# Stack loads of a two-pass attention kernel split by heads into two groups

## The reference

```
q_rot, k_rot = _rotate(q, cos, sin), _rotate(k, cos, sin)          # 16 heads of 8 channels
scores = einsum('bhqd,bhkd->bhqk', q_rot, k_rot) / sqrt(8) + decay_bias
scores = where(causal, scores, -inf)
attn = softmax(scores); out = einsum('bhqk,bhkd->bhqd', attn, v) @ Wo.T
```

## Time and profile before

| what | value |
|---|---|
| median of 3 runs | 1439.15 us (1437.37 to 1440.41) |
| profiled execution | 1432.54 us, span 1430.7 us |
| TensorE busy | 1284.3 us (90%) |
| VectorE busy | 1021.5 us (71%) |
| ScalarE busy | 762.4 us (53%) |
| GpSimd busy | 221.6 us (15%) |
| share of the 16 DMA engines, queue q1 | 32.6% |
| granted TensorE clock, mean | 0.984 of 2.4 GHz |

### The profile page before, as it was taken

One profiled execution on the slowest core, in us unless ns is written; L12 is line 12 of the kernel. 1 busy time (PEld: TensorE's weight loads), 2 busy tenths in 40 slices (PEclk: granted clock), 3 DMA queues, 4 the chain that ended last, 5 costly groups with the idle time before them and its releaser, 6 DMA issues.

```text
span 1430.7 us, 33751 instructions
## 1 busy us (share of the span) xinstructions
PE 1284.3 (90%) x10686; PEld 1016.5 (71%) x10780; DVE 1021.5 (71%) x3882; ACT 762.4 (53%) x1664; POOL 221.6 (15%) x326
## 2 busy tenths in 40 slices
PE   0369999999999999999999999999999979999999
PEld 0247777777778777777777777777777767777776
DVE  8557777777777777777777777777776656677754
ACT  1125655665555555555555555555555574455532
POOL 4011112111122211111111111112111200000000
PEclk9679999999999999999999999999999999999999
DMA  4423233223333333333222233223223204554344
GB/s 117 94 54 85 76 77 76 75 76 80 79 85 79 78 76 79 83 90 90 77 75 76 75 83 80 76 75 76 75 76 77 58 9 172 204 202 153 149 153 159
DMA packets 89904, 133.33 MB, mean 93 GB/s; under 512 B 9675, under 2 KB 78395, under 8 KB 78523
## 3 DMA queue, kind: packets, MB, share of 16 engines
q1 hardware_dynamic: 89298, 132.10, 32.6%
q10 hardware_dynamic: 488, 0.01, 0.0%
HBM read 108.76 MB, written 21.50 MB: 91 GB/s over the span
## 4 chain that ended last, share of the span: by engine, by line
PE 63%; DVE 15%; DMA 11%; issue 6%; ACT 4%; DVEq 1%; SPq 0%; ACTq 0%
DMA qst<-mT 10%; PE ps L1663 8%; PE ps L1649 8%; PE ps L1401 7%; PE ps L1402 6%; PE ps L1411 6%; PE ps L1275 4%; PE ps L1379 4%; DVE mx L1025 3%; PE ps L1337 3%; PE ps L1360 3%; PE ps L1333 2%; PE ps L1330 2%; PE ps L1436 1%; PE ps L1383 1%
## 5 line engine op out<-in xcount | busy, mean ns | idle before, releaser
L629 ACT ACTIVATE pr<-ps 128x512 f32<-128x512 f32 x384 | 227.7, 593 | 205.4 <-PE ps L1360 166.7
L1025 DVE TENSOR_REDUCE mx<-ps 128x2 f32<-128x512 f32 (+1 forms) x384 | 263.9, 688 | 46.6 <-PE ps L1330 26.2
L634 ACT ACTIVATE ps<-trn 128x512 f32<-128x512 bf16 x382 | 229.8, 601 | 12.1
L530 POOL TENSOR_TENSOR n1s<-rep,n1T 128x256 f32<-128x256 f32 x256 | 177.0, 730 | 277.4 <-DVE mpart L1037 252.9
L1663 PEld LDWEIGHTS ps<-w2s,ats 128*128 128x128 f32 x1024 | 131.7, 192 | 50.4 <-issue 46.5
L1401 PE MATMUL ps<-n1s,wq 128*128 128x256 f32 x512 | 160.6, 396 | 0.0
L1402 PE MATMUL ps<-n1s,wk 128*128 128x256 f32 x512 | 152.8, 380 | 0.0
L1411 PE MATMUL ps<-wv,n1s 128*128 128x128 f32 x1024 | 150.6, 280 | 0.0
L803 ACT ACTIVATE n1s<-ps 128x512 f32<-128x512 f32 x128 | 76.5, 597 | 123.3 <-PE ps L1649 122.1
L1411 PEld LDWEIGHTS ps<-wv,n1s 128*128 128x128 f32 x1024 | 131.9, 192 | 9.0 <-issue 6.3
L1663 PE MATMUL ps<-w2s,ats 128*128 128x128 f32 x1024 | 135.7, 276 | 1.1 <-DVE ats L1207 1.1
(11 more groups left out here) (225 smaller groups left out, 2281.6 us busy)
## 6 DMA issues: line engine op xcount, KB each, us to landing
rep<-scr_rw SPq DMA_DIRECT2D x32, 1024.0 KB, 5.0
qst<-scr_rw SPq DMA_DIRECT2D x16, 1024.0 KB, 6.5
kst<-scr_rw SPq DMA_DIRECT2D x16, 1024.0 KB, 8.3
scr_parts<-parts SPq DMA_DIRECT2D x64, 192.0 KB, 2.3
qst<-scr_parts SPq DMA_DIRECT2D x192, 64.0 KB
kst<-scr_parts SPq DMA_DIRECT2D x32, 192.0 KB
xt<-in_x SPq DMA_DIRECT2D x32, 128.0 KB, 2.3
kst<-scr_parts SPq DMA_DIRECT2D x32, 128.0 KB
```

Of the source, the lines that this page charges most:

```text
L530: pool.tensor_tensor(n1s[:, e], rep[:, par, e], n1T[:, par], ALU.mult).then_inc(n1s_done, 1)
L629: act.activation(pr[:, G % 2, i], ps[:, S2[k % 2]], ACT.Exp).then_inc(exp_done, 1)
L634: act.activation(ps[:, S2[k % 2]], seeds[:, 1 if (k + 2) % 3 == 2 else 0], ACT.Copy).then_inc(seed_done, 1)
L1025: dve.tensor_reduce(mx[:, min(i, 1), h:h + n], ps[:, S1[k % 2]].rearrange("p (h t) -> p h t", h=n), AX_X, ALU.max, negate=True).then_inc(s ...
```

## The change

`stacks` gets an argument `half` and issues the ten DMAs for 8 of the 16 heads. It is called twice in a row: for half 0 it waits until 6 units of pass 2 of batch n are done, for half 1 until all 12 are. Each half counts on a semaphore of its own; `unit1` waits for half 0 at unit 0 and for half 1 at unit 6. All rows of a load are 4 KB now. Nothing is changed in what the other engines do.

```diff
 Q_SLOTS = ((0, 1, 0), (1, 1, 0), (2, 1, 0), (3, 1, 1), (4, 1, 1), (5, 1, 2))
 K_SLOTS = ((0, 3, 0), (3, 2, 0), (5, 1, 0))
 KR = P
+HALF_HEADS = H // 2
 STACK_DMAS = 1 + len(Q_SLOTS) + len(K_SLOTS)
 LN2_LINKS = 3 + 10
...
         rot_chain = sem("rot_chain")
         parts_out = sem("parts_out")
         parts_stored = sem("parts_stored")
-        stack_in = sem("stack_in")
+        stack_in = [sem("stack_lo_in"), sem("stack_hi_in")]
         v_out = sem("v_out")
         v_done = sem("v_done")
         s1_out = sem("s1_out")
...
                     sp_.dma_start(scr_parts[par, side].rearrange("p d h t -> (d h) p t"),
                                   parts[:, :, side]).then_inc(parts_stored, 16)
-            def stacks(b, par, old):
+            def stacks(b, par, old, half):
+                hh = slice(HALF_HEADS * half, HALF_HEADS * (half + 1))
                 if old:
-                    sp_.wait_ge(s2_out, UNITS * (b - 1))
-                sp_.dma_start(qst[R_MAX:R_MAX + 3, par], zeros_b[:].broadcast_to((3, H, S))).then_inc(stack_in, 16)
+                    sp_.wait_ge(s2_out, UNITS * (b - 2) + UNITS // 2 * (half + 1))
+                sp_.dma_start(qst[R_MAX:R_MAX + 3, par, hh], zeros_b[:].broadcast_to((3, HALF_HEADS, S))
+                              ).then_inc(stack_in[half], 16)
                 sp_.wait_ge(parts_stored, 32 * (b + 1))
                 for side, dst, slots in ((0, qst, Q_SLOTS), (1, kst, K_SLOTS)):
-                    v = scr_parts[par, side].rearrange("p d h t -> (p d) (h t)")
+                    v = scr_parts[par, side].rearrange("p d h t -> (p d) h t")
                     for first, n, part in slots:
-                        rows = dst[R_PARTS + DH * first:R_PARTS + DH * (first + n), par].rearrange("p h t -> p (h t)")
-                        sp_.dma_start(rows, v[DH * part:DH * (part + n)]).then_inc(stack_in, 16)
+                        rows = dst[R_PARTS + DH * first:R_PARTS + DH * (first + n), par, hh]
+                        sp_.dma_start(rows, v[DH * part:DH * (part + n), hh]).then_inc(stack_in[half], 16)
             def store_weights(b, par):
...
                 if n_x >= 2:
                     store_parts(n + 2, u)
                 if n_x >= 2:
-                    stacks(n + 2, u, True)
+                    stacks(n + 2, u, True, 0)
+                    stacks(n + 2, u, True, 1)
                     store_weights(n + 2, u)
                 if n_x:
                     put_max(n + 1, 1 - u)
             store_parts(0, 0)
-            stacks(0, 0, False)
+            stacks(0, 0, False, 0)
+            stacks(0, 0, False, 1)
             store_weights(0, 0)
             spread_weights(0, 0)
...
             sp_.wait_ge(x_in, 32)
             load_x(2, 0, xt, x_in)
             store_parts(1, 1)
-            stacks(1, 1, False)
+            stacks(1, 1, False, 0)
+            stacks(1, 1, False, 1)
             store_weights(1, 1)
             put_max(0, 0)
             step(0, 0, 3)
...
                     pe.wait_ge(rwT_done, b + 1 if not isinstance(b, int) or b else 2)
                 if k == 0:
-                    pe.wait_ge(stack_in, 16 * STACK_DMAS * (b + 1 if not isinstance(b, int) or b else 2))
+                    pe.wait_ge(stack_in[0], 16 * STACK_DMAS * (b + 1 if not isinstance(b, int) or b else 2))
+                if k == UNITS // 2:
+                    pe.wait_ge(stack_in[1], 16 * STACK_DMAS * (b + 1 if not isinstance(b, int) or b else 2))
                 if k == 0:
                     pe.wait_ge(mT_done, b)
```

## The result

The changed kernel takes 1394.6 us (median of 4 runs, 1393.7 to 1394.73) where the kernel before, run beside it, took 1438.26 (1435.13 to 1440.41): a ratio of 0.9714, 95% interval [0.9692, 0.9736], 43.7 us less. The forecast was 1411, with a range that ended at 1403. The direction and the place were right; the gain was 28 us in the forecast and 43.7 in fact. Later groups of runs of the kernel before had medians of 1434.4 to 1437.3, so some 4 of the 43.7 us can be scatter of that kernel; against the lowest of them the gain is 39.8.

What follows compares the result with a forecast made beforehand. TensorE, busy 90%, bounds the kernel, with idle time before pass 2 while `put_max` waits behind stack loads. Gains of 26.0 (loop) and 2.0 (start) make 28.0 us, taking the median 1439.15 to 1411; range 1403 to 1424.

Steps and rivals of the forecast that it cites:

- Item 1, the mechanism: End of pass 2: with half the stack bytes left there, their tail ends before `put_max` is issued, hiding its landing.
- Item 1, the size: TensorE's wait ahead of pass 2: 28 steps at 0.93 us each, a gain of 26.0 us; ends 0 and 26.
- the two steps that I used as steps without a stop: Loop steps of 33.31 and 33.05 us, read as without idle time, 0.96 shorter than the average 34.14.
- Item 2: Low half's earlier issue on SP: its waits and loads fit in 4.3 us of idle queue; cost 0.
- Item 3: TensorE's waits in `unit1` for the two halves: both landed a step earlier in the steady loop; cost 0.
- Item 4, the start: Pass 1 of batch 0 waits for the low half alone: gain of 2.0 us taken, ends 2.4 gain and 2.4 loss.
- The sum: Whole kernel: 26.0 + 2.0 = 28.0 us gain; profiled execution 1432.54 becomes 1404.5, median 1439.15 becomes 1411.
- the 6.6 us: Excess of the kernel before's three-run median, 1439.15 us, over its profiled execution; its place was not seen.
- A: Rival: the tail shrinks less or another late thing takes half the gap; 13 us gain, 1426 us; chance 0.08.
- B: Rival: stack-load time is per load, not per byte, so `put_max` lands as now; forecast 1440 us; chance 0.07.
- C: Rival: SP's issue of loads cut by heads gets dearer, delaying `put_max`; 17 us more, 1456 us; chance 0.05.
- The rule that speaks against it: Stack loads: transfers under 64 KB are dominated by per-descriptor cost, so 32 KB loads would bring the sum near 0.

Runs made afterwards that it cites:

- the second trace of before: The kernel before, unchanged, profiled once more: profiled execution 1436.01 us, median of nine runs 1434.42 us.
- the run made for it: Kernel before with twelve whole, late stack loads, each load's rows spread six partitions apart: 1446.23 us, ratio 1.0087.

## Why the prediction was right and wrong

- *Item 1, the mechanism.* Right. The tail of the stack loads held `put_max`; half of the bytes end before it is issued; TensorE's idle time fell by 26.5 us for the 26.0 forecast (0.4 of it in the first step). The run from ScalarE's queue, the cut at 4 heads and the early issue taken away say the same from three sides; the last of them adds that bytes count only while they are under way.
- *Item 1, the size.* This is a step that failed: "Gain: 28 x 0.93 = 26.0 us" took a stop to cost its idle time only; the term measured 34.4. After a stop the engine also fills again, as I call it. Part of that stands ahead of pass 2. In the kernel before (first row) the last pair starts 0.94 us ahead of pass 2, which comes at 673.52; in the changed kernel (second row) it starts 0.22 ahead of 685.20. That is a loss of 0.72 where the idle time noted is 0.56:

```profile
672.58 0.38 PE L1267 MATMUL ps<-ident,zt 128*128 128x128 f32 x2
...
684.98 0.38 PE L1273 MATMUL ps<-ident,zt 128*128 128x128 f32 x2
```

  In the chain the whole of it shows. Before, the chain counts 0.39 and 0.50 us for pass 2's first pair and the next (L1360, L1401); without a stop 0.22 and 0.43:

```profile
673.52 0.39 PE ps L1360 x2
673.91 0.50 PE ps L1401 x2
```

```profile
685.36 0.22 PE ps L1369 x2
685.58 0.43 PE ps L1410 x2
```

  The first fence is the chain of the kernel before, the second that of the changed one. That is 0.24 us beside the idle time here, and 0.31 on the average over the steps with a gap: some 8 to 9 us in all. Of the two steps that I used as steps without a stop only the one of 33.05 was one. The one of 33.31 has a short stop that the waits view does not put down to `qst<-mT`:

```profile
400.36 0.10 issue
400.46 0.39 PE ps L1360 x2
```

  Its first pair counts 0.39, as behind any stop. So my sentence that these two had no idle time is wrong for one of them. (The step of 33.29 in the second trace of before counts 0.27 and 0.62 in the same places.) The 0.96 that I got from their mean looked like a confirmation of 0.93 and stopped me from looking; with 33.05 alone it would have been 1.09.
- *Item 2.* Right: 4.9 us of cover for the 4.3 forecast, cost 0.
- *Item 3.* Right: no wait of TensorE on either half in the loop.
- *Item 4, the start.* Right in kind, 2.85 for 2.0, with 0.4 of the 2.85 from a shorter wait for the first `put_max`. Undoing TensorE's wait costs 2.3 between medians, near the 2.4 that was the upper end, but 0.3 between the traces at the first like point. The forecast left out the granted clock, which moved in this stretch. The loss that I set against it did not come; `store_weights` went out 4.4 us later (58.14 for 53.76), and yet the 1 MB load came at 60.44, before the 61.29 of the earlier trace rows, as that store now landed in 2.29 us.
- *The sum.* The second step that failed: "with the same gain it becomes 1411". The profiled execution of before, 1432.54, was one of its quicker ones, below all four runs of the comparison, and the changed kernel's profiled execution, 1394.73, is 0.1 above its median. The gain between the two, 37.8 us, is 5.9 short of the gain between medians. I had noted that the 6.6 us could be this wait and put 8 into the foot of the range for it; that is of the size of what came, the 9 us of refilling were missing, and 1394.6 lies below the foot of 1403.
- *The rivals.* A and B did not come. C did not either, but its price is real: 0.64 to 0.70 us of issue for a load in the runs whose loads lost the plain shape.
- *The rule that speaks against it.* The Trainium skill (DMA: Bandwidth & Descriptors, "Bandwidth") has transfers under 64 KB dominated by a price per descriptor. This case does not agree: the loads of half the size (32 KB and, into `kst`, up to 96) moved 404 KB in 4 us, 101 GB/s, where those of the kernel before had 138 GB/s at first and 67 in their tail.

What stays open: why the stacks drain at about 100 GB/s when `rep` moves at 347. Shorter rows are not the cure; neighbouring partitions and the 8 engines remain, and the run made for it was decided by SP's issue instead.

## What to carry to other kernels

A small transfer on the path waits for the bytes that are still under way when it is issued, so count what is issued in the microseconds before it; move bulk loads to the moment when their buffer comes free, part by part, and look first at which waits let you do it. When a wait is removed, count the refill of the engine with each stop, and when the kernel before scatters from run to run, the gain between medians can be larger than what a quick profile shows. Keep the shape of a load plain while splitting it, since issue time on a queue is a price too.

## What was unexpected of the hardware

- A stop of TensorE in front of pass 2 costs 0.31 us beside its idle time (mean of 49 steps in two traces, 0.19 to 0.44 in single ones; 0.24 in the step shown).
- The issue of an 8-row load costs SP 0.36 to 0.37 us whatever the row (2, 4 or 8 KB), but 0.70 with two pieces a row and about 0.65 with partitions six apart.
- `put_max` waits as long from ScalarE's queue as from SP's (33.8 us of idle time against 29.0 and 31.2).
- 768 KB given in 7.3 us are through within 1 to 2 us of the last issue (131 GB/s in the first microsecond after it, 22 in the next); given in 3.3 us they leave a tail of some 5 us (90 GB/s still in 670 to 671), and end no sooner after the first load (some 9 us for both).
